# A four-layer graph network on one core: the set-up stage laid out anew, and a new order of steps

## The reference, cut to what matters

```
L0: e = u1[idx1] + u2[idx2]; leaky 0.1; masked softmax over axis 1; att @ h + x @ self_weight
L1: GAT (leaky 0.2, masked softmax) -> layernorm, relu -> A @ h + (1+eps) h -> two-layer MLP with a layernorm
L2: GAT with softmax over the neighbours, + bias, ELU
L3: A = softmax(where(adj > 0, e[cumsum(adj) - 1], NEG)); diag(A) * (x @ W0) + (A - diag) @ (x @ W1) + bias
```

## Time and profile before

| | us |
|---|---|
| median of 3 runs | 1051.17 (1049.97 to 1051.28) |
| the profiled execution's own time | 1053.7 |
| its span | 1052.0 |
| PE busy in the span | 964.9 (92%) |
| DVE busy | 873.9 (83%) |
| ACT busy | 629.9 (60%) |
| POOL busy | 554.2 (53%) |

### The profile page before, as it was taken

The page is one execution under the profiler, slowest core; times in us unless marked ns, Lnnn a source line. Parts: engine busy times, 40 slices in busy tenths (PEclk is TensorE's granted clock), DMA queues, the critical chain, the costliest instruction groups (busy, mean ns, idle before and its releaser), DMA issues. The chain is left out here.

```text
span 1052.0 us, 21202 instructions
## 1 busy us (share of the span) xinstructions
PE 964.9 (92%) x7355; PEld 913.3 (87%) x7355; DVE 873.9 (83%) x2532; ACT 629.9 (60%) x1641; POOL 554.2 (53%) x1169
## 2 busy tenths in 40 slices
PE   4788999998999999999989899999899999997996
PEld 4678998988999889998988899898899999886996
DVE  5978797899868888897989878689998888778873
ACT  2444556676677664667574764676537775677631
POOL 3425344574558662665565554547436655465840
PEclk8778899999999899999999999999999999999999
DMA  6020000000011010002000101100100100000004
GB/s 137 2 59 2 2 2 1 2 1 2 1 41 41 2 41 2 2 9 73 2 1 1 41 1 41 41 1 2 41 2 2 40 2 2 1 2 1 1 1 121
DMA packets 38490, 20.17 MB, mean 19 GB/s; under 512 B 3184, under 2 KB 37872, under 8 KB 38384
## 3 DMA queue, kind: packets, MB, share of 16 engines
q1 hardware_dynamic: 36512, 18.42, 6.6%
q10 hardware_dynamic: 1872, 0.40, 0.2%
HBM read 10.43 MB, written 8.39 MB: 18 GB/s over the span
## 5 line engine op out<-in xcount | busy, mean ns | idle before, releaser
L639 PE MATMUL ps<-HE,PT 128*128 128x129 f32 x2048 | 240.5, 277 | 5.9 <-issue 4.8
L639 PEld LDWEIGHTS ps<-HE,PT 128*128 128x128 f32 x2048 | 234.7, 193 | 9.3 <-issue 7.9
L925 ACT ACTIVATE Y<-X,SM 128x128 f32<-128x128 f32 x512 | 203.9, 490 | 44.8 <-POOL SM L1083 44.8
L1291 DVE SCALAR_TENSOR_TENSOR PT<-ps,CE,maskT 128x512 f32<-128x512 f32 x256 | 174.1, 742 | 12.2 <-PE ps L763 5.4
L1068 POOL TENSOR_TENSOR SM<-ST 128x8 f32<-128x8 f32 x96 | 32.0, 333 | 276.6 <-DVE ST L1154 276.5
L1079 POOL TENSOR_TENSOR SM<-SM,minus_half 128x8 f32<-128x8 f32 x96 | 162.2, 1690 | 7.6
L639 PE MATMUL ps<-W,HT 128*128 128x128 f32 (+1 forms) x768 | 126.5, 312 | 1.7 <-ACT HT L918 1.6
L639 PEld LDWEIGHTS ps<-W,HT 128*128 128x128 f32 x768 | 116.1, 194 | 11.2 <-ACT HT L918 2.0
L1154 DVE BATCH_NORM_STATS2 ST<-X 128x6 f32<-128x128 f32 x512 | 104.9, 278 | 16.8 <-DMA X<-in_x_dram 13.7
L656 PE MATMUL ps<-ident,Y 128*128 128x128 f32 x640 | 86.2, 280 | 10.1 <-ACT Y L925 8.0
L656 PEld LDWEIGHTS ps<-ident,Y 128*128 128x128 f32 x640 | 74.0, 145 | 14.2 <-ACT Y L925 12.8
(11 more groups left out here) (262 smaller groups left out, 2356.6 us busy)
## 6 DMA issues: line engine op xcount, KB each, us to landing
X<-in_x_dram SPq DMA_DIRECT2D x32, 256.0 KB, 3.5
out_dram<-X SPq DMA_DIRECT2D x32, 256.0 KB, 2.8
adj_raw<-in_adj_dram SPq DMA_DIRECT2D x4, 256.0 KB, 3.7
W<-in_L_gnn_W_dram SPq DMA_DIRECT2D x1, 128.0 KB, 5.7
Ws<-n_L_gnn_self_weight_dram ACTq DMA_DIRECT2D x1, 64.0 KB, 3.3
W<-in_L_gnn_W_dram ACTq DMA_DIRECT2D x1, 64.0 KB, 3.6
feat2w<-in_L_gnn_W_dram ACTq DMA_DIRECT2D x1, 64.0 KB, 4.2
Wo<-L_gnn_others_weight_dram SPq DMA_DIRECT2D x1, 64.0 KB, 5.6
```

The costliest lines, as they stand in the source:

```text
L639: return nc.tensor.matmul(o, w, m, start=start, stop=stop, skip_group_check=True)
L925: a = A(dst[:, n, 0:F], src[:, n, 0:F], func, scale=SM[s][:, S_RSTD, n:n + 1], bias=SM[s][:, S_SHIFT, n:n + 1])
L1291: a = V.scalar_tensor_tensor(out=PT[r][:, j, :], in0=o, scalar=CE[s][:, c:c + 1], in1=maskT[:, j, :].bitcast(F32), op0=ALU.max, op1=ALU.mult)
```

## The change

- The 27 small loads become three sets with a semaphore each: `WEIGHTS` (10) and `VECTORS` (9), both issued by ACT in that order, and `REST` (11), issued by SP behind all six loads of `X0`, `X1`, `X2`. Three bias rows are loaded to the two partitions that need them, not to 128.
- PE starts the transposes of the mask when the identity is there. It takes the three weight transposes next, behind `WEIGHTS` alone. The 16 one-column products of L484 go; `off_col` comes from four one-column products with `off_b` at the end.
- ACT copies the transposed mask in eight pieces with an accumulating output, which gives the column counts; the two big sums on DVE go. ACT takes over three copies from DVE.
- The ranks (`erank`) leave `PREP`: PE computes them at the end of the set-up, ACT copies them out in two pieces.
- `stat0` and `scale0` of groups 0 and 1 (`EARLY` = 2) are done inside the set-up, on DVE, POOL and ACT; POOL also does the addition on `bias3`, behind `REST`.
- All strings of `TURNS` and `HOMES` are written anew. On PE 247 of the 469 common steps stand at another place, by 0.9 places on average; on DVE 264 of 469, by 1.2. PE's order of the first steps is now `0:norm0 eoffm eedge ecover evalue 1:norm0 1:coef0 0:coef0 0:cmax0 2:norm0 1:cmax0 0:feat0 1:feat0 0:coefb0 eturn 2:coef0 1:coefb0 2:cmax0 2:feat0 0:agg0 0:self0 1:agg0`; before, `2:feat0` stood behind `1:agg0`. SP's string loads group 4 before 3 and 5 (before: 3, 5, 4), and ends in `15:load 10:store 14:store 13:store 12:store 11:store 15:store`. Groups 4 and 3 stay in this order in DVE's `stat0`, ahead of `1:coefb0` and `1:split0`.

```diff
+EARLY = 2
...
-    ("erank", 4, "pe act"),
...
-    "sp": ("354100617228394a5b6c7d8e9fedcbaf"),
...
+    "sp": ("4350261728394a5b6c7d8e9faedcbf"),
...
+        POOL_SETUP = 14
+        POOL_IDENT = 10
...
+            todo = [(name for name, _, engines in steps if e in engines.split()) 
+                    for steps in [STEPS[3:]] * EARLY + [STEPS] * (GROUPS - EARLY) + [PREP]]
...
+        WEIGHTS = [(Wo[:], Wo_d), (feat1w[:, 0:F], Wp_d), (feat2w[:, 0:F], Wq_d),
+                   (att0[:, 0:1], att0_d[0:P, :]), (att0[:, 1:2], att0_d[P:2 * P, :]),
+                   (asd[:, 0:1], column(asrc_d)), (asd[:, 1:2], column(adst_d)),
+                   (att2[:, 0:1], att2_d[0:P, :]), (att2[:, 1:2], att2_d[P:2 * P, :]), (bpcol[:], column(bp_d))]
+        VECTORS = [(brow[p0:p0 + 1, k, :], v.partition_broadcast(1)) for p0 in (0, 32)
+                   for k, v in enumerate((bp_d, b1_d, b2_d))] + [
+                   (epscol[:], eps_d.partition_broadcast(P)),
+                   *[(e_col[:, m:m + 1], column(e_d[0, m * P:(m + 1) * P])) for m in range(MB)]]
+        REST = [(Ws[:], Ws_d), (W1[:], W1_d), (W2[:], W2_d), (W3[:], W3_d.rearrange("k f g -> f k g")),
+                (mlp_g[:], column(mlpg_d)), (mlp_b[:], column(mlpb_d)), (e255[:], e_d[0, NE - 1:NE].partition_broadcast(P)),
+                (bias3[:], bias3_d.partition_broadcast(P)), (bias2[:], bias2_d.partition_broadcast(P)),
+                (gat_g[:], gatg_d.partition_broadcast(P)), (gat_b[:], gatb_d.partition_broadcast(P))]
...
-                for s in range(1):
+                for s in range(NS // 2):
                     for b in range(G):
                         sp.dma_start(X[s][:, b::G, :],
                                      x.rearrange("b (t p) f -> b p t f", p=P)[s * G + b]).then_inc(x_loaded[s], 16)
-                for dst, src in LOADS[0::2]:
-                    sp.dma_start(dst, src).then_inc(loaded, 16)
-                for s in range(1, NS // 2):
-                    for b in range(G):
-                        sp.dma_start(X[s][:, b::G, :],
-                                     x.rearrange("b (t p) f -> b p t f", p=P)[s * G + b]).then_inc(x_loaded[s], 16)
+                for dst, src in REST:
+                    sp.dma_start(dst, src).then_inc(loaded["rest"], 16)
 
...
+                sp.wait_ge(loaded["rest"], 16 * len(REST))
...
+                for s in range(EARLY):
+                    pool.wait_ge(sig["var"][s], 1)
+                    rstd_of(pool, link, s, False).then_inc(sig["rstd"][s], 1)
+                pool.wait_ge(loaded["rest"], 16 * len(REST))
+                nc.gpsimd.tensor_scalar(bias3[:], bias3[:], -1.0, None, ALU.add)
...
-                pe.wait_ge(made["pool"], POOL_SETUP)
-
+                pe.wait_ge(made["pool"], POOL_IDENT)
                 for j in range(T):
                     for i in range(T):
                         o = (j % 2) * N + i * P
                         mm = T_(ps[j // 2][:, o:o + P], adjn[:, i, j * P:(j + 1) * P].bitcast(F32), ident[:])
-                mm.then_inc(made["turn"], 1)
-
+                    if j % 2 == 1:
+                        mm.then_inc(made["turn"], 1)
+
+                pe.wait_ge(loaded["weights"], 16 * len(WEIGHTS))
+                for n, w in enumerate((Wo, feat1w, feat2w)):
+                    mm = T_(ps[2][:, N + n * P:N + (n + 1) * P], w[:, 0:F], ident[:])
+                mm.then_inc(made["WT_ps"], 1)
+
+                pe.wait_ge(made["pool"], POOL_SETUP)
                 pe.wait_ge(made["counts"], 1)
...
-                        MM(ps[2][:, 16 + i:17 + i], strict[:, k, i * P:(i + 1) * P].bitcast(F32), cnt_row[:, k:k + 1],
-                           start=(k == 0), stop=(k == T - 1))
                 for k in range(T):
                     mm = MM(ps[3][:, N:2 * N], cntrep[:, k, :], strict[:, k, :], start=(k == 0), stop=(k == T - 1))
                 mm.then_inc(made["off"], 1)
-
-                pe.wait_ge(loaded, 16 * len(LOADS[0::2]))
-                pe.wait_ge(loaded_too, 16 * len(LOADS[1::2]))
-                for n, w in enumerate((Wo, feat1w, feat2w)):
-                    mm = T_(ps[2][:, N + n * P:N + (n + 1) * P], w[:, 0:F], ident[:])
-                mm.then_inc(made["WT_ps"], 1)
...
 
+                for i in range(T):
+                    for j in range(T):
+                        mm = MM(ps[i // 2][:, (i % 2) * N:(i % 2 + 1) * N], maskT[:, j, i * P:(i + 1) * P],
+                                upper[:, j, :], start=(j == 0), stop=(j == T - 1))
+                    if i % 2 == 1:
+                        mm.then_inc(made["rank"], 1)
+                pe.wait_ge(made["off_b"], 1)
+                for i in range(T):
+                    mm = MM(ps[2][:, N + 400 + i:N + 401 + i], off_b[:, i * P:(i + 1) * P], ident[:, 0:1], start=True, stop=True)
+                mm.then_inc(made["off_col"], 1)
...
                 A = nc.scalar.activation
-                for dst, src in LOADS[1::2]:
-                    act.dma_start(dst, src).then_inc(loaded_too, 16)
-                act.wait_ge(made["turn"], 1)
-                A(maskT[:, 0:2, :], ps[0][:].rearrange("p (a n) -> p a n", a=2), ACT.Copy)
-                A(maskT[:, 2:4, :], ps[1][:].rearrange("p (a n) -> p a n", a=2), ACT.Copy).then_inc(made["maskT"], 1)
+                for dst, src in WEIGHTS:
+                    act.dma_start(dst, src).then_inc(loaded["weights"], 16)
+                for dst, src in VECTORS:
+                    act.dma_start(dst, src).then_inc(loaded["vectors"], 16)
+                for h in range(2):
+                    act.wait_ge(made["turn"], h + 1)
+                    for k in (2 * h, 2 * h + 1):
+                        for c in range(2):
+                            n = c * (N // 2)
+                            o = (k % 2) * N + n
+                            a = A(maskT[:, k, n:n + N // 2], ps[h][:, o:o + N // 2], ACT.Copy,
+                                  accum_out=cnt_half[:, k, c:c + 1])
+                    a.then_inc(made["maskT"], 1)
                 act.wait_ge(made["WT_ps"], 1)
                 for n, w in enumerate((WoT, WpT, WqT)):
                     a = A(w[:], ps[2][:, N + n * P:N + (n + 1) * P], ACT.Copy)
                 a.then_inc(made["WT"], 1)
-                act.wait_ge(made["maskT"], 1)
+                act.wait_ge(made["off"], 1)
+                A(off_b[:], ps[3][:, N:2 * N], ACT.Copy).then_inc(made["off_b"], 1)
+                act.wait_ge(made["maskT"], 2)
                 A(gin_hi[:], maskT[:].bitcast(F32), ACT.Copy).then_inc(made["gin_hi"], 1)
-                act.wait_ge(loaded_too, 16 * len(LOADS[1::2]))
+                for s in range(EARLY):
+                    if s == 1:
+                        act.wait_ge(made["rowtot"], 1)
+                        A(rowtot_b[:], ps[3][:, 0:N], ACT.Copy)
+                        for h in range(2):
+                            act.wait_ge(made["rank"], h + 1)
+                            A(rank[:, 2 * h:2 * h + 2, :], ps[h][:].rearrange("p (a n) -> p a n", a=2), ACT.Copy)
+                    act.wait_ge(sig["rstd"][s], 1)
+                    scaled(Y[s], X[s], s, ACT.Relu).then_inc(sig["normed"][s], 1)
 
...
+                def first_stats(s):
+                    dve.wait_ge(x_loaded[s], 16 * G)
+                    for n in range(TG):
+                        a = V.bn_stats(ST[s][:, n, :], X[s][:, n, :])
+                    a.then_inc(sig["var"][s], 1)
+
                 dve.wait_ge(adj_loaded, 16 * T)
                 V.tensor_scalar(adjn[:], adj_raw[:], 0.0, None, ALU.is_gt).then_inc(made["adjn"], 1)
-                dve.wait_ge(made["pool"], POOL_SETUP)
                 dve.wait_ge(made["adjn"], 1)
-                V.tensor_copy(m_row[:], m_int[:])
-                V.tensor_copy(m_col[:], mc_int[:])
                 link(V.reduce_sum(cnt_row[:], adjn[:].bitcast(F32), AX_X))
                 V.tensor_scalar(norow[:], cnt_row[:], 0.0, None, ALU.is_equal)
+                dve.wait_ge(made["pool"], POOL_SETUP)
                 for k in range(T):
                     a = V.tensor_scalar(cntrep[:, k, :], ones[:], cnt_row[:, k:k + 1], None, ALU.mult)
                 a.then_inc(made["counts"], 1)
+                first_stats(0)
+                dve.wait_ge(loaded["weights"], 16 * len(WEIGHTS))
+                V.tensor_tensor(asum[:], asd[:, 0:1], asd[:, 1:2], ALU.add)
...
+                V.tensor_copy(m_col[:], mc_int[:])
+
+                dve.wait_ge(made["maskT"], 2)
                 mT = maskT[:].bitcast(F32)
-                V.reduce_sum(cnt_low[:], mT[:, :, N // 2:N], AX_X)
...
                 v8 = [t[:].rearrange("p (k b) -> p k b", b=G) for t in (low8, empty8, full8, share8)]
...
+                first_stats(1)
+
+                dve.wait_ge(made["wvec"], 1)
+                V.tensor_copy(wv[:, 6:7], ps[2][:, 390:391])
+                link(V.tensor_copy(wv[:, 0:6], ps[2][:, 384:390]))
...
+                dve.wait_ge(loaded["vectors"], 16 * len(VECTORS))
...
 ```

(27 more changed lines are left out.)

241 lines of the change are left out of this document (106 added, 135 removed).

## The result

The changed kernel takes 1035.39 us (median of 4 runs, 1034.39 to 1035.80), the kernel before 1051.22 beside it (4 runs): a ratio of 0.9845, interval 0.9824 to 0.9865, or 15.8 us less. The forecast was 1044.8, 6.4 less, and its range ended at 1038.5: the sign is right, the size is 9.4 us short. The profiled execution took 1035.57, with a span of 1033.8.

The account below looks back on a forecast made before the run. PE, busy 95% from 100 to 1040 us, was taken as the bound. Three quarters of -6.1 us at 90 us (-4.6) plus -1.8 for stores gave -6.4, so 1044.8 us; 8 in 10 within 1038.5 to 1051.5.

Parts of the forecast that it names:

- Set-up: Start, up to the wait of all engines: ACT comes out last, second block begins at 29.0 instead of 31.64; -2.6 us.
- the rule in the Trainium skill: Set-up: weight loads share engines with X0 to X2, PE's weight transposes slip 1 us; sum -5.6 instead of -6.4.
- erank's cover: Second block's start to eedge: without erank PE idles, then runs at low clock; +2.0 us, bounds 0 and 2.6.
- the forecast sum of -0.6: Running sum up to eedge: -2.6 us for the set-up and +2.0 for the lost cover of erank.
- The order from 58 to 90: 58 to 90 us: 2:feat0 fills the gap before 0:agg0, -2.6; loading group 4 first shortens 1:agg0's gap, -2.9.
- the 6.1 of the forecast: Total lead forecast at 90 us: -0.6 - 2.6 - 2.9 = -6.1 us.
- Stores: After PE's last product: ten stores remain in a row instead of twelve, -1.8 us in full; bounds 0 and -1.8.
- How much is left at the end: From 90 us to the end: three quarters of the 6.1 us lead stays, -4.6 us; bounds 0 and all.
- All carries: Whole kernel: ranks hold the clock up, nothing is given back; -9.9 us, 1041.3 (1038 to 1042); chance 0.24.
- absorbed: Steady stretch: DVE and ACT set PE's waits, only the stores' gain stays; -1.8 us, 1049.4; chance 0.18.
- the ACT stall: Set-up: SP's X loads hold up ACT's issue by up to 9.6 us; +3.2 us, 1054.4; chance 0.08.
- the worse order: Steady stretch: new order adds four more 25 us stretches with PE idle 5.0; +8.1 us, 1059.3; chance 0.10.

Follow-up runs that it names:

- e9: The changed kernel itself, measured and profiled again in a later batch; ratio 0.983 to the kernel before.
- f2: The changed kernel itself, measured and profiled once more in a later batch; 1035.36 us, ratio 0.9838 to the kernel before.
- e1: Changed kernel's set-up with the step order and banks of before (less erank and the first norms of groups 0 and 1); 1054.84 us, ratio 0.9999.
- e5: Changed kernel with group 10's store again behind those of 14, 13, 12 and 11; 1037.0 us, ratio 0.983.
- e3: Changed kernel with its new order only up to about 125 us, then the order of before; 1051.55 us, ratio 0.9964.
- e7: Changed kernel with 2:feat0 put back behind 1:agg0 on PE, its banks moved with it; 1037.59 us, ratio 0.9823.
- e6: Changed kernel with SP's loads again in the order 3, 5, 4; 1037.56 us, ratio 0.9837.
- e4: Changed kernel's set-up, the order of before up to about 125 us, then the new order; 1040.07 us, ratio 0.9867.
- m3: e1 with 10:norm2 moved before 12:agg0 on PE alone, each with its banks; 1053.79 us, ratio 1.0015.

## Why the forecast was wrong

- *Set-up, -2.6.* Measured -3.6, the block at 28.02. The chain was the right one (ACT ends it, its last Y at 27.56, forecast 28.6). The ranks were mis-sized: 3.92 us, not the 6.57 of the earlier trace rows. PE came into them busy (3.8 of the 4 us before) and they ran at a granted clock of 1.00, where the earlier trace rows has 0.55. ACT's loads ended at 10.2, not 11.3; the eight copies took 3.0 us in all (forecast 3.2). ACT did have to wait before its first `scale0`, 1.67 us for POOL, whose chain took 5.0 and not 4.0. SP's last small load landed at about 18.6, 4.9 us after its issue (the forecast put `REST` at 26, and counted twelve small loads on SP before where the trace has 14). By the forecast's working from the rule in the Trainium skill (DMA: Bandwidth & Descriptors, "Issuing engines are not separate DMA queues"), PE's weight transposes would have come 1 us late. They ran at 12.51 with no wait, so this did not come about; the rule itself, that such loads share the 16 DMA engines, no run here puts to the test.
- *erank's cover, +2.0.* Right in kind: PE idles 3.73 us and works at 0.50. Too small in size: the clock costs 3.4 us, above the bound of 2.6, since the 16 small products of `eoffm` (3.57 us instead of 1.84) were left out. Before, `eoffm` had to wait for the end of `erank`, which gives 0.7 back. The head start shrinks by 2.7 us, from 3.6 to 0.9; that the forecast sum of -0.6 is met within 0.4 is in part luck, for the set-up gave 1 more than forecast.
- *The order from 58 to 90, -5.5.* Right in kind, and rather too small. 1:agg0 starts 6.0 us earlier than in the earlier trace rows, which looks like the 6.1 of the forecast, but that sum counts `2:feat0` as already done: in its terms 1:agg0 would have started only 3.5 earlier (in e9 and f2 it is 5.3 and 4.8). By work the lead is 8.7 us at 135 us in this profile, 7.3 and 6.0 in e9's and f2's (e1, with the old order, has 3.1 there). With the gaps went a low clock (0.50 before, 1.00 after at 1:agg0), for which the forecast had no term.
- *Stores, -1.8.* Met: 1.5, and e5 undoes just that (1.8).
- **How much is left at the end: this is the step that failed.** "Nothing before 1040 waits for a fixed time ... Bounds 0 and all ... I take three quarters" treats all between 90 and 1040 us as something that passes on or swallows a lead. What share of a lead from the start reaches the end was not measured cleanly: e3 keeps 3.8 us of 8.5, but lost most of the rest at its cut; e1 keeps nothing of 3 (give or take 2); by one profile each, e7's part is lost and e6's kept. But the new order of that stretch has a value of its own, which the forecast set at nothing, and for which it had only a rival that makes it worse. The runs put 14.8 us there (e1 less e4), 1.5 of them the stores. In the traces of those two the last products lie 16.4 apart: 5.5 won up to 4100 products ahead, 6 up to 3600 (most of it a low clock in e1's profile, below), 12 up to 2100, then 0.6 lost up to 600 and 6.7 behind that. In the changed kernel itself, against before, it is 8: of the 18.1 us between the two spans 8.7 were there at 135 us (forecast 6.1), 7.9 came behind it (forecast -1.5) and 1.5 are the stores.
- *The rivals.* "All carries" (1041.3), the highest of the gains, lies 6 us above the time; "absorbed", the ACT stall and the worse order are out. The stall did not come: SP issued its six X loads in 5.8 us, and ACT had all 19 of its own issued by 10.2. The sign of "worse order" was right for the last 90 us and wrong for the rest. The argument against it, "the mean move is one place", holds for neither sign: moves of about one place took away 8.6 us of idle time in 180 us.

The evidence was in the earlier trace rows: 50.6 us of PE idle time between 100 and 1040 in a change that rewrites every string. What the new order would make of them could not be read there, but that a good part might go could, and the range kept no room for it: its low end, 1038.5, was worked out from the visible edits alone. Part of what went came back elsewhere: up to its last product the changed kernel idles 46.2 us behind 100 us, 4.4 less. The other 3.5 or so of the 7.9 us are busy time, an estimate from the 12.2 us by which PE is less busy there and the 8.7 of the lead.

Still open: which moved steps of DVE, ACT or POOL, or which banks, take away the waits of the middle. m3 shows only that this one move in PE's list alone does not.

## What to carry to other kernels

When a change rewrites a hand-written order, take the idle time of the bounding engine over the whole rewritten part into the range, on both sides, however small the moves look (here 50.6 us, of which 4.4 went in the end: 8.6 less in one stretch of 180 us, more at the end); the visible edits at the start may be the smaller part. Compare traces by work left (products still ahead), not by time: the stretches then show each its own gain or loss, which the total hides, and a better end can be grafted on. Cut two orders only where every engine has issued the same steps in both, and look for a new wait at the cut before you read the time.
